# A two-layer gated cross-attention kernel: part of the second layer's gate weights moved to ScalarE, and an output sum rewritten as two strided reductions

## The reference, cut to what matters

```python
xn = x / norm(x);  sn = sim_matrix / norm(sim_matrix, axis=0)
logits = xn @ sn - sigmoid(gates)                 # 16 experts
gated = relu(logits);  hard = gated > 0
inactive = (sum(hard, axis=1) == 0)               # an idle token: no expert above zero
put = inactive * one_hot(top_2(logits))           # it gets its two best experts
masked = where(mask_with(put) > 0, gated, -inf)
w = softmax(masked)                               # gate weights, 16 per token
q, k, v = (sum_e w[:, e] * (x @ proj[e]) for proj in (q_proj, k_proj, v_proj))
o = softmax(q @ k.T / sqrt(128)) @ v              # within a sequence
out = sum_e w[:, e] * (o @ o_proj[e])
```

## Time and profile before

| what | value |
|---|---|
| median of 3 runs | 1622.75 us (1621.93 to 1623.85) |
| the profiled execution | 1619.88 us, its span 1618.2 us |
| mean granted TensorE clock | 0.977 |
| PE busy over the span | 1499.3 us, 93% |
| DVE, POOL, ACT busy | 1285.3 us (79%), 1186.7 us (73%), 1103.2 us (68%) |
| layer two's steps | from about 566 us to the end |

### The profile page before, as it was taken

The page is one execution under the profiler, slowest core; times in us unless marked ns, Lnnn a source line. Parts: engine busy times, 40 slices in busy tenths (PEclk is TensorE's granted clock), DMA queues, the critical chain, the costliest instruction groups (busy, mean ns, idle before and its releaser), DMA issues.

```text
span 1618.2 us, 52841 instructions
## 1 busy us (share of the span) xinstructions
PE 1499.3 (93%) x17129; PEld 1304.2 (81%) x17130; DVE 1285.3 (79%) x4046; ACT 1103.2 (68%) x2757; POOL 1186.7 (73%) x1715
## 2 busy tenths in 40 slices
PE   6888888866999789999999999999999999999996
PEld 4666666646999479888888888888888889889985
DVE  4777777754555378988999989988998999988885
ACT  4888888843556457677676776677667766776664
POOL 4666666632455568888888888888888888888785
PEclk9999999977999899999999999999999999999998
DMA  3221222225543000000000000000000000000000
GB/s 81 86 65 65 65 65 65 79 83 130 146 137 85 27 15 15 21 15 15 21 20 16 15 21 16 20 15 21 15 22 15 17 19 21 15 15 18 5 7 11
DMA packets 85963, 64.84 MB, mean 40 GB/s; under 512 B 11888, under 2 KB 81552, under 8 KB 85776
## 3 DMA queue, kind: packets, MB, share of 16 engines
q1 hardware_dynamic: 70368, 45.13, 9.6%
q0 software_dynamic: 5120, 12.62, 2.5%
q10 hardware_dynamic: 10288, 4.74, 1.1%
HBM read 35.74 MB, written 22.52 MB: 36 GB/s over the span
## 4 chain that ended last, share of the span: by engine, by line
PE 80%; issue 7%; DVE 6%; POOL 2%; ACT 2%; DMA 1%; SPq 0%; POOLq 0%; DVEq 0%; ACTq 0%
PE s_bank L2016 12%; PE s_bank L2018 11%; PE s_bank L2017 11%; PE tb L1833 7%; PE s_bank L1951 4%; PE po L1963 4%; PE s_bank L1813 4%; PE po L1847 3%; PE m L1784 2%; PE s_bank L2164 2%; PE s_bank L1822 1%; PE m L1863 1%; DVE qkv L1567 1%; PE m L1767 1%; PE s_bank L2151 1%
## 5 line engine op out<-in xcount | busy, mean ns | idle before, releaser
L746 POOL TENSOR_TENSOR qkv<-qkv,scaled 128x384 f32<-128x384 f32 x480 | 489.3, 1019 | 85.3 <-ACT scaled L1032 36.1
L1032 ACT ACTIVATE scaled<-s_bank,wg 128x384 f32<-128x384 f32 x449 | 260.2, 584 | 114.7 <-PE s_bank L2018 110.1
L2016 PE MATMUL s_bank<-proj_hi,hn_hi 128*128 128x384 f32 x900 | 327.3, 364 | 5.4 <-DVE qkv L1567 5.4
L1567 DVE SCALAR_TENSOR_TENSOR qkv<-s_bank,wg,qkv 128x384 f32<-128x384 f32 x449 | 273.7, 610 | 51.0 <-PE s_bank L2018 41.0
L2018 PE MATMUL s_bank<-proj_hi,hn_lo 128*128 128x384 f32 x900 | 302.5, 336 | 0.0
L2017 PE MATMUL s_bank<-proj_lo,hn_hi 128*128 128x384 f32 x900 | 301.6, 335 | 0.0
L900 ACT ACTIVATE pT<-tb 128x512 f32<-128x512 f32 x256 | 154.6, 604 | 111.2 <-PE tb L1833 110.5
L1833 PE MATMUL tb<-ident,prob 128*128 128x128 f32 x1024 | 162.9, 283 | 46.3 <-issue 30.5
L2016 PEld LDWEIGHTS s_bank<-proj_hi,hn_hi 128*128 128x128 f32 x900 | 169.5, 188 | 18.8 <-DVE qkv L1567 14.0
L1833 PEld LDWEIGHTS tb<-ident,prob 128*128 128x128 f32 x1024 | 119.6, 145 | 71.3 <-issue 63.1
L2017 PEld LDWEIGHTS s_bank<-proj_lo,hn_hi 128*128 128x128 f32 x900 | 170.0, 189 | 1.6
(11 more groups left out here) (288 smaller groups left out, 3753.5 us busy)
## 6 DMA issues: line engine op xcount, KB each, us to landing
xs<-sorted_in SPq DMA_DIRECT2D x71, 128.5 KB, 2.1
sorted_out<-yo SPq DMA_DIRECT2D x71, 64.0 KB, 1.6
xin<-in_x SPq DMA_DIRECT2D x32, 128.0 KB, 2.1
cin<-in_ctx SPq DMA_DIRECT2D x32, 128.0 KB, 2.4
ctx_cols<-xcT SPq DMA_DIRECT2D x32, 128.0 KB, 1.8
w<-in_L_ffn_W SPq DMA_DIRECT2D x16, 256.0 KB
xcT<-ctx_cols SPq DMA_DIRECT2D x32, 128.0 KB, 2.8
kx<-kT SPq DMA_DIRECT2D x128, 32.0 KB
```

What stands on the lines that cost most here:

```text
L746: g.tensor_tensor(into, into, scaled[m % SCALED][:, 0:cols], ALU.add).then_inc(dense_added, 1)
L1032: ins = act.activation(into, bank[:, 0:3 * D], ACT.Copy, scale=wg[v % 4][:, 1, k:k + 1])
L1567: v.scalar_tensor_tensor(out=acc, in0=bank[:, 0:3 * D], scalar=wg[w % 4][:, 0, k:k + 1], in1=acc, op0=ALU.mult, op1=ALU.add).then_inc(dens ...
L2016: pe.matmul(bank[:, 0:cols], hi[:, tile], of(proj_hi), start=True, stop=False)
```

## The change

It has three pieces. First, the shift by the maximum is no longer an operation of VectorE: `gtop` is stored negative and is the bias of ScalarE's exponential, now one instruction per tile, on the logits without relu (where a logit is not above zero the mask makes the product zero). Second, the pairs of idle tokens are no longer added to the mask but to the masked exponentials, so `gate_mask` goes and an addition in `gate_select` comes; `gate_both` and `gate_idle` are moved from behind q14 to behind q10; selection, sum and reciprocal are moved from behind o3 to behind q15; the multiplication by the reciprocal goes to ScalarE, two instructions of 128x16 between its parts o1 and o2. Third, the output sum: `total_groups` becomes one reduction of four groups of `sums` straight into `oall[:, 1]`, `total` one reduction of two groups of `halves` into `oall[:, 0]`; `result` comes ahead of `total_groups`.

```diff
-                    act.activation(ex[:, :, :], lg[:, :, :], ACT.Exp).then_inc(f["wexp_ready"], 1)
+                    for t in range(2):
+                        ins = act.activation(ex[:, t, :], lg[:, t, :], ACT.Exp, bias=gtop[:, t:t + 1])
+                    ins.then_inc(f["wexp_ready"], 1)
+
+            def gate_weights(v):
+                if exists(v):
+                    act.wait_ge(f["gate_ready"], v + 1)
+                    w = wg[v % 4]
+                    for t in range(2):
+                        ins = act.activation(w[:, t, :], w[:, t, :], ACT.Copy, scale=gate[:, t:t + 1])
+                    ins.then_inc(f["w_ready"], 1)
...
                 take(u, "o", 0, 1)
+                gate_weights(u + 1)
                 apply_norm(1, u + 4, u % 2)
...
-            GATE = 17
+            GATE = GATE_STEPS   # 15
...
             def gate_floor(step):
-                step.free(v.tensor_scalar(gtop[:, :], top[:, :, 0], 0.0, None, ALU.max))
-            def gate_shift(step):
-                step.wait(9)
-                v.scalar_tensor_tensor(out=lg[:, :, :], in0=lg[:, :, :], scalar=0.0, in1=bcast(gtop[:, :], E1, 2),
-                                       op0=ALU.max, op1=ALU.subtract).then_inc(s[1]["logits_ready"], 1)
+                v.tensor_scalar(gtop[:, :], top[:, :, 0], 0.0, -1.0, ALU.max, ALU.mult)\
+                    .then_inc(s[1]["logits_ready"], 1)
...
-            def gate_mask(step):
-                step.wait(13)
-                step.free(v.tensor_tensor(gm[:, :, :], gm[:, :, :], fb[:, 0, :, :], ALU.add))
             def gate_select(u, step, w):
                 v.wait_ge(f["wexp_ready"], u + 1)
+                step.free(v.tensor_tensor(w[:, :, :], ex[:, :, :], gm[:, :, :], ALU.mult))
+                step.wait(13)
+                step.free(v.tensor_tensor(w[:, :, :], w[:, :, :], fb[:, 0, :, :], ALU.add))
...
-                v.tensor_tensor(w[:, :, :], w[:, :, :], bcast(gate[:, :], E1, 2), ALU.mult)\
-                    .then_inc(f["w_ready"], 1)
+                v.reciprocal(gate[:, :], den[:, :]).then_inc(f["gate_ready"], 1)
...
             def total_groups(w):
-                    v.tensor_tensor(halves[:, 1, :, :], sums[:, 0:2, :], sums[:, 2:4, :], ALU.add)\
+                    wait(v, f["res_ready"], w)
+                    v.tensor_reduce(oall[:, 1, :], sums[:, :, :].rearrange("p g n -> p n g"), AX_X, ALU.add)\
                         .then_inc(f["sum_steps"], 1)
             def total(w):
-                    v.wait_ge(f["sum_steps"], 2 * w + 1)
-                    v.tensor_tensor(oall[:, :, :], halves[:, :, 0, :], halves[:, :, 1, :], ALU.add)\
+                    v.tensor_reduce(oall[:, 0, :], halves[:, :, :].rearrange("p g n -> p n g"), AX_X, ALU.add)\
                         .then_inc(f["sum_steps"], 1)
...
                 take(u, "q", 3, 4)
+                result(u - 3)
                 total_groups(u - 2)
-                result(u - 3)
                 token_weights(u - 1)
...
                     gate_index(gates)
                     gate_floor(gates)
-                    gate_shift(gates)
                     gate_pairs(gates)
+                    gate_both(gates)
+                    gate_idle(gates)
                 take(u, "q", 11)
...
                 take(u, "q", 13, 14)
+                take(u, "q", 15)
                 if exists(u + 1):
-                    gate_both(gates)
-                    gate_idle(gates)
-                    gate_mask(gates)
-                take(u, "q", 15)
+                    gate_select(u + 1, gates, wg[(u + 1) % 4])
+                    gate_sum(gates, wg[(u + 1) % 4])
+                    gate_divide(gates)
                 take(u, "o", 0)
...
                 take(u, "o", 2, 3)
-                if exists(u + 1):
-                    gate_select(u + 1, gates, wg[(u + 1) % 4])
-                    gate_sum(gates, wg[(u + 1) % 4])
-                    gate_divide(gates)
-                    gate_weights(gates, wg[(u + 1) % 4])
```

More of the change, by code:

```diff
@@ L32 @@
 EXPS = (0, 1, 2, 3)
+GATE_STEPS = 15
 LOWER_MAXIMA = (0, 1, 3, 2)
@@ L248, in flamingo @@
         sums = sb("sums", [P, 4, D])
-        halves = sb("halves", [P, 2, 2, D])
+        halves = sb("halves", [P, 2, D])
         oall = sb("oall", [P, 2, D])
@@ L290, in flamingo @@
         split_done = sem("split_done")
-        fnames = ("nrm_steps", "nrm_ready", "gate_steps", "gate_logits", "wexp_ready", "w_ready",
+        fnames = ("nrm_steps", "nrm_ready", "gate_steps", "gate_logits", "wexp_ready", "gate_ready", "w_ready",
                   "first_keys", "hn_lo_ready", "oh_lo_ready", "qk1_in_psum", "qk1_ready", "s1_in_psum",
@@ L1112, in _ @@
             apply_norm(1, 3, 1)
+            gate_weights(0)
             upper_units(act, body1)
@@ L1485, in gate_both, with gate_sum @@
             def gate_both(step):
-                step.wait(11)
+                step.wait(10)
                 step.free(v.tensor_tensor(fb[:, 0, :, :], fb[:, 0, :, :], fb[:, 1, :, :], ALU.add))
             def gate_idle(step):
-                step.wait(12)
+                step.wait(11)
                 step.free(v.tensor_tensor(fb[:, 0, :, :], fb[:, 0, :, :], bcast(idle[:, :], E1, 2), ALU.mult))
-            def gate_mask(step):
-                step.wait(13)
-                step.free(v.tensor_tensor(gm[:, :, :], gm[:, :, :], fb[:, 0, :, :], ALU.add))
             def gate_select(u, step, w):
                 v.wait_ge(f["wexp_ready"], u + 1)
+                step.free(v.tensor_tensor(w[:, :, :], ex[:, :, :], gm[:, :, :], ALU.mult))
+                step.wait(13)
+                step.free(v.tensor_tensor(w[:, :, :], w[:, :, :], fb[:, 0, :, :], ALU.add))
+            def gate_sum(step, w):
                 step.wait(14)
-                step.free(v.tensor_tensor(w[:, :, :], ex[:, :, :], gm[:, :, :], ALU.mult))
-            def gate_sum(step, w):
-                step.wait(15)
                 step.free(v.tensor_reduce(den[:, :], w[:, :, :], AX_X, ALU.add))
             def gate_divide(step):
-                step.wait(16)
-                step.free(v.reciprocal(gate[:, :], den[:, :]))
-            def gate_weights(step, w):
-                step.wait(17)
+                step.wait(15)
                 step.end()
-                v.tensor_tensor(w[:, :, :], w[:, :, :], bcast(gate[:, :], E1, 2), ALU.mult)\
-                    .then_inc(f["w_ready"], 1)
+                v.reciprocal(gate[:, :], den[:, :]).then_inc(f["gate_ready"], 1)
             def max_bank(w, j):
@@ L1572, in take_part @@
                         for e in range(4 * k, 4 * k + 4):
-                            into, cols = halves[:, 0, e % 2, :], slice(D * (e % 4), D * (e % 4) + D)
+                            into, cols = halves[:, e % 2, :], slice(D * (e % 4), D * (e % 4) + D)
                             if e < 2:
@@ L1705, in _ @@
             gate_divide(gates)
-            gate_weights(gates, wg[0])
             upper_units(v, body1)
```

## The result

The changed kernel takes 1629.54 us, the median of 5 runs (1627.55 to 1631.81), against 1622.75: a ratio of 1.0036, with a 95% interval of 1.0024 to 1.0048. The forecast was 1630.0 us. The profiled execution took 1627.55 us (before 1619.88), its span is 1625.8 us (before 1618.2). The sum to explain is +7.7 us in the profile, +6.8 in the medians.

The account below looks back on a forecast made before the run. TensorE was taken to bound the kernel, so gains come only where it waits for VectorE. The median 1622.75 plus 28 x 0.26 = 7.3 us for ScalarE, all else 0, gave 1630.0 us; range 1618 to 1653.

Parts of the forecast that it names:

- ScalarE's cost: Two multiplications between o1 and the norm delay the next masks by 0.26 us a step, 7.3 us (2.8 to 10.6) in all.
- the hand-over from o3 to the masks: From ScalarE's o3 end to TensorE's mask load: 0.23 us at most, so ScalarE can be 0.14 us late without harm.
- The first reduction: `total_groups` as strided reduction ahead of q5: 0.68 to 1.10 us in place of 0.41, taken as cost 0.
- The cover by GpSimd's addition: Line 1546, ahead of q5, waits for GpSimd's addition anyway; this 1.36 us long cover hides the first reduction's delay.
- start and end, together 0: First step -0.2 to +0.4 us, end +0.27 to +0.69 us, less 0.4 for `result`; taken as 0.
- second rival: Line 1546's cover fails: first reduction delays q5, 9 to 21 us, 1639 to 1651 us with ScalarE's cost; chance 0.06.
- first rival: A margin at the pairs ahead of q11 is lost, the heads' division is held, TensorE waits for `oT`: 1652 us; chance 0.25.
- The boundary between steps: Selection, sum and reciprocal leave the place behind o3, where VectorE waits for scores: 0 either way, at worst 0.2 us.
- Second reduction and pairs: `total` ahead of the heads: 0.41 to 0.62 us in place of 0.71; pairs ahead of q11: q11 0.12 us later, cost 0.
- the margins of 0.02 and 0.06 us: At the pairs, the second comparison and `gate_idle` issue just ahead of GpSimd's additions by these amounts, so neither is caught.

Follow-up runs that it names:

- e1: The kernel before with the two strided reductions alone and `result` ahead of `total_groups`, gates as before; ratio 1.0020.
- e4: The changed kernel with ScalarE's weight multiplications issued ahead of part o0 instead of behind o1; ratio 1.0001 to the kernel before.
- e5: The changed kernel with the first reduction reading four neighbouring elements at a time instead of strided, so its output is wrong; 1632.39 us, one time.
- e2: The changed kernel with the old output sums in the old order, so the gate pieces alone; ratio 1.0021 to the kernel before.
- e10: The kernel before with `result` alone moved ahead of the first maximum; ratio 0.9988.
- e12: e6 with `result` moved ahead of the first maximum; ratio 0.9977 to the kernel before.
- e6: e2 with ScalarE's weight multiplications ahead of part o0, so both gate pieces with the old sums; ratio 0.9994 to the kernel before.
- e3: The changed kernel with the multiplication of the weights back on VectorE, behind the reciprocal ahead of part o0; ratio 1.0030 to the kernel before.
- e7: e4 with `result` and `total_groups` moved behind part q5; ratio 1.0049 to the kernel before.
- e11: e9 with `total` moved from ahead of the heads to behind part q14; 1612.47 us, ratio 0.9919 to the kernel before.
- e9: e4 with `result` moved ahead of the first maximum and `total_groups`, the reduction, behind part q5; ratio 1.0013 to the kernel before.
- e8: The kernel before with `total_groups` and `result` moved behind part q5, nothing else; ratio 1.0091.

## Why the prediction was right, and where it was not

**The total** (1630.0 forecast, 1629.54 measured) is right, its one term only by mechanism. The forecast was 7.3 us for ScalarE and 0 for all else. The runs show about 4.5 for ScalarE and 3.7 for the sums by themselves (e1), of which the gates' move gives back some 1.5 us behind the last mask load. What is left of the 7.7 us in the profile, above all the 1.0 ahead of the steps, isn't shown to come from the change. That the forecast of the total is off by 0.5 us only is luck: one term was 2.8 us too high, and terms put at 0 made up for it.

**ScalarE's cost.** The two multiplications took 0.40 us, the estimate to the digit. The slack was mis-sized. I put the hand-over from o3 to the masks at 0.23 us, the lowest that a trace showed, called it "at most", and then used it as the value: 0.37 - 0.23 = 0.14. It is 0.11, so the slack is 0.26, the stall 0.40 - 0.26 = 0.14, and the weight load shows nearly that (0.40 instead of 0.25 us of idle time). Over the 28 mask loads the waits add up to 11.0 us instead of 7.0. The whole step was 0.17 longer (e4), so 0.03 more was lost than the masks show; I haven't traced that. I had foretold that the profile would name ScalarE's line 1036 as what the load waits for; it names "issue", as before.

**The first reduction.** Priced at 0.68 to 1.10 us, it took 1.09, the bound from the earlier trace rows; e5 shows that the stride makes the difference. The cover by GpSimd's addition held in the regular steps: line 1546 shrank from 1.65 to 0.73 us and ended as foretold. It failed in the one step with a late gather (+0.58 us). What failed as a term is "start and end, together 0". The cover is a gather and the addition behind it; where units have run out there is no gather, line 1546 isn't held as long (0.60 us before, in the last step), and a reduction longer by 0.69 us makes it late, so late that it loses to GpSimd's next addition. That is the second rival's mechanism with the first rival's on top. The prediction priced the end once, at +0.27 to +0.69 us, and set `result`'s 0.4 us against it; it comes in the last step and three times behind it. e1 has its price: 0.7 us in the last step and 3.2 behind it, ahead of the clock's fall.

**The boundary between steps.** The prediction said that the gate operations behind o3 were not on the path, since VectorE goes on to wait for the scores. That holds while there are scores. At the two boundaries behind the last mask load there are none: TensorE waited 1.02 and 1.49 us for part q0 in the kernel before, and now waits 0.51 us for ScalarE. It is a gain of 1.5 us that the prediction had at 0, and in e2, where the sums are the old ones, other waits take it back.

**A gain that I had at 0.** With `result` out of the way of the second gather the step is 0.06 shorter (e1 and e10 against before, e12 against e6). Rows of before and after show where: the second gather takes 1.09 us in one and 1.01 in the other. In before, e2 and e6 `result` starts about 0.29 us ahead of that gather and is still running when it begins; there it takes 1.06 to 1.10 us in nearly all steps. In after, e1, e3, e4, e7, e10, e11 and e12 no two-input operation of VectorE lies across its start (but for one step of e11), and it takes 1.01 to 1.02. GpSimd's addition then ends 0.07 earlier, and line 1546 with it.

**Second reduction and pairs.** 0.42 us for the second reduction, the lower end of 0.41 to 0.62; the pairs went as written, operation by operation: in the 26 steps from the mask load at 632.68 on, all but the last, the comparisons take 0.18 us and the multiplication by `idle` 0.19, so the margins of 0.02 and 0.06 us held. The first rival (0.25) did not occur in the changed kernel, which has no wait for `oT` at all. Its mechanism is in the kernel before, once (the division held for 1.26 us, TensorE's wait 0.7), and e9 shows that its mechanism and its size are real: 0.06 us on the wrong side of GpSimd costs 0.54 us of VectorE and up to 0.7 of TensorE's wait, 0.6 us a step.

**The lock and the reductions.** In the last step the reduction at 1493.44 runs beside GpSimd's addition from 1493.53 and takes 1.10 us, against 1.09 beside a gather: it isn't caught. The rule of the Trainium skill that I cited for this ("SBUF — State Buffer", section "Who interferes with whom") holds here. The note of the Trainium skill on SBUF cachelines on the same page gives a penalty for every access to a new line of 16 bytes and no size. The four-way reduction agrees, 1091 ns against 686; the two-way one doesn't, with 424 ns for 256 elements against 412 contiguous, and there the measurement decides.

## What to carry to other kernels

Cost a small instruction by the slack of the queue it joins: two multiplications of 0.2 us were free ahead of o0 and cost 4.5 us behind o1, in the same queue 2.6 us later. When a cost is hidden by work of another engine, list the steps in which that work is missing or comes late, the last ones above all, and price them apart; the same steps can hold gains, where a wait that covered an operation is gone. An operation that shares VectorE's and GpSimd's lock should be placed against the start of the other side's instruction, and each move re-checked at the next such pair: here e7, e8 and e9 only shifted the wait, and e11 removed it.

## What the runs showed of the hardware

- A gather of GpSimd doesn't hold a two-input operation of VectorE from its very start. Line 1546 issued 0.03 us into it ran freely (e7, 0.42 us), and so it did up to 0.10 us into it (e1, one step); from 0.35 us on it was held until the addition behind had ended as well (e10, 0.38 us into it: 1.98 us). But in the first step with a gather beside it, line 1546 was issued 0.37 to 0.40 us into it and took 0.42 us, in ten of the kernels (before: issued at 608.19, the gather began at 607.82). So the time since the gather's start doesn't decide alone, and what else does isn't known.
- The other way round, a two-input operation of VectorE that is running when the gather begins makes the gather about 0.07 us longer (1.08 against 1.01 us).
- An operation held while the gather runs isn't let through between the gather and GpSimd's next addition (0.01 to 0.04 us later): it waits out both.
- A reduction over four rows 512 bytes apart takes 1091 ns for 512 elements, over neighbours 686; over two rows there is no such difference.
- ScalarE multiplies 128x16 elements by a scale from memory in 0.32 us, but two in a row occupy its queue for 0.40.
- TensorE's weight load can follow 0.11 us behind the ScalarE instruction that it needs.
